# A decoder of four layers: row maxima of two attention cores taken one group and three tiles ahead of the scores, not two groups

## The reference, cut to what matters

```python
scores = einsum('bhqd,bhkd->bhqk', q, k) / sqrt(16)       # 512 x 1024 a head
weights = softmax(scores, axis=-1)
ctx = einsum('bhqk,bhkd->bhqd', weights, v)
```

## Time and profile before

| | us |
|---|---|
| median of three runs | 4876.44 (4870.0 to 4876.64) |
| the profiled execution | 4892.19 |
| its span in the trace | 4890.3 |
| `l1x_core`, first maxima to last exponential | 1498.9 to 1905 |
| `l3x_core`, first maxima to last exponential | 4262.6 to 4782 |
| granted TensorE clock, mean | 0.903 |

### The profile page before, as it was taken

The page is one execution under the profiler, slowest core; times in us unless marked ns, Lnnn a source line. Parts: engine busy times, 40 slices in busy tenths (PEclk is TensorE's granted clock), DMA queues, the critical chain, the costliest instruction groups (busy, mean ns, idle before and its releaser), DMA issues. The chain is left out here.

```text
span 4890.3 us, 69700 instructions
## 1 busy us (share of the span) xinstructions
PE 4176.7 (85%) x20384; PEld 1980.6 (41%) x20384; DVE 2875.0 (59%) x6517; ACT 2350.6 (48%) x4572; POOL 1358.3 (28%) x1202
## 2 busy tenths in 40 slices
PE   8679857689788997797988999999998988489986
PEld 6322346377552333483234333333335544222224
DVE  4458574401667884103863378777873256388866
ACT  4337331243233775233664455454552246279993
POOL 0122141212101111111220288787883212101112
PEclk9669978699887999898898999999999999689998
DMA  8445212354133332574335521111210034613421
GB/s 287 114 104 124 57 38 35 128 198 146 40 117 72 67 69 66 201 255 150 78 75 198 186 69 61 62 62 61 76 44 35 10 117 97 150 47 93 99 52 38
DMA packets 332043, 486.58 MB, mean 99 GB/s; under 512 B 84516, under 2 KB 232597, under 8 KB 317253
## 3 DMA queue, kind: packets, MB, share of 16 engines
q1 hardware_dynamic: 321552, 443.63, 32.1%
q0 software_dynamic: 6384, 32.61, 2.2%
q10 hardware_dynamic: 3804, 6.74, 0.4%
HBM read 327.63 MB, written 143.92 MB: 96 GB/s over the span
## 5 line engine op out<-in xcount | busy, mean ns | idle before, releaser
L1391 POOL TENSOR_TENSOR lc_totals<-lc_totals,lc_weights 128x1024 f32<-128x1024 f32 (+1 forms) x320 | 622.9, 1946 | 164.6 <-DVE lc_totals L1340 133.9
L1321 DVE TENSOR_REDUCE lc_part_max<-ps 128x2 f32<-128x1024 f32 x384 | 466.4, 1215 | 222.1 <-PE ps L1166 219.6
L1300 ACT ACTIVATE lc_weights<-ps 128x1024 f32<-128x1024 f32 x384 | 392.9, 1024 | 418.3 <-PE ps L1186 405.0
L1186 PE MATMUL ps<-lc_q,lc_k 64*128 64x512 f32 x1536 | 395.9, 594 | 4.8 <-issue 4.8
L1196 PE MATMUL ps<-lc_weights,lc_v 128*64 128x512 f32 x1536 | 371.8, 605 | 0.0
L866 DVE TENSOR_REDUCE l1x_core_part_max<-ps 128x1 f32<-128x512 f32 x512 | 316.6, 682 | 55.3 <-PE ps L690 55.1
L862 DVE CUSTOM_DVE_ANT_0 l3x_core_unused<-ps,l3x_core_mask_q 128x512 f32<-128x512 f32 x512 | 330.6, 686 | 6.9 <-DVE l3x_core_row_max L870 4.9
L825 ACT ACTIVATE l3x_core_weights<-ps 128x512 f32<-128x512 f32 x512 | 327.0, 693 | 7.6 <-PE ps L758 7.2
L825 ACT ACTIVATE l1x_core_weights<-ps 128x512 f32<-128x512 f32 x512 | 266.1, 604 | 84.1 <-PE ps L758 84.0
L808 ACT ACTIVATE ps<-l3x_core_mask_k 128x512 f32<-128x512 f32 x384 | 270.2, 704 | 35.8 <-DMA l3x_core_mask_k<-in_mask_k 35.8
L690 PE MATMUL ps<-l3x_core_k,l3x_core_q 96*128 96x512 bf16 x512 | 213.9, 419 | 55.0 <-DVE l3x_core_part_max L862 39.9
(11 more groups left out here) (494 smaller groups left out, 8582.3 us busy)
## 6 DMA issues: line engine op xcount, KB each, us to landing
cf_w<-in_L1f_w SPq DMA_DIRECT2D x32, 1024.0 KB, 7.4
lc_k<-latent_k SPq DMA_DIRECT2D x32, 768.0 KB
lc_v<-latent_values SPq DMA_DIRECT2D x32, 768.0 KB, 5.0
latent_k<-feed_staged SPq DMA_DIRECT2D x64, 256.0 KB, 2.4
latent_values<-feed_staged SPq DMA_DIRECT2D x64, 256.0 KB, 2.0
k_heads<-proj_parts SPq DMA_DIRECT2D x40, 384.0 KB, 2.6
q_heads<-proj_parts SPq DMA_DIRECT2D x32, 384.0 KB, 2.6
q_heads<-proj_parts SPq DMA_DIRECT2D x32, 256.0 KB, 3.0
```

Of the source, the lines that this page charges most:

```text
L1186: mm = nc.tensor.matmul(out[j], k_tile[g % RING][strip(j), i * P:(i + 1) * P], q_tile[g % RING][strip(j), :], start=False, stop=True)
L1300: nc.scalar.activation(weights[:, i % TILES, :, :], k.ps[:, B0 + (i % 2) * HEADS:B0 + (i % 2 + 1) * HEADS, 0:nq], ACT.Exp, scale=scale).th ...
L1321: nc.vector.reduce_max(own, k.ps[:, A0:A0 + HEADS, :], AX).then_inc(a_taken, 1)
L1391: nc.gpsimd.tensor_tensor(total, total, own, ALU.add).then_inc(added_by_pool, 1)
```

## The change

`EARLY = 3` for these two stages: `FRONT` is 12 chunks (3 tiles' worth), `TURN` is tile 5. Before the first score the 32 chunks of group 0 and 12 of group 1 are done. At step s of group g chunk 12 + s of group g + 1 follows for s below 20, and chunk s - 20 of group g + 2 from there. The turn of group g + 1 moves from the end of tile 0 to step 22, and negate to step 23; split and `row` move to the end of GpSimd's and SyncE's program for the group. The loads of the mask by queries move from group 1 to group 2 of a batch, and `row` stands before the last of the four loads of the mask by keys in group 3. All other stages run the same instructions in the same order.

```diff
+    EARLY = 3 if small and nkt == 8 else nkt
+    late_row = EARLY < nkt
+    FRONT, TURN = NCH * EARLY // nkt, nkt - EARLY
+
+    def chunks_at(s):
+
+        return [(1 + m // NCH, m % NCH) for m in range(FRONT + s * NCH // NS, FRONT + (s + 1) * NCH // NS)]
...
-                if exists(*later(b, g, 1)):
+                if exists(*later(b, g, 1)) and not late_row:
                     row(*later(b, g, 1))
...
-                if mask is not None and g == groups - 3 and exists(b + 1, 0):
+                if mask is not None and g == groups - (2 if late_row else 3) and exists(b + 1, 0):
                     for qi in range(nqt):
                         sync.wait_ge(a_taken, at(b, groups - 1, NCH + 1, (qi + 1) * NCH // nqt))
                         load_mask_q(b + 1, qi)
...
+                new_mask = mask is not None and g == groups - 1 and exists(b + 1, 0)
+                for i in range(nkt // 2 if new_mask else 0):
+                    if late_row and i == nkt // 2 - 1:
+                        row(*later(b, g, 1))
+                    sync.wait_ge(exp_done, at(b, g, NS, 2 * (i + 1) * heads + 3))
+                    load_mask_k(b + 1, i)
+                if exists(*later(b, g, 1)) and late_row and not new_mask:
+                    row(*later(b, g, 1))
...
-            pass_a(0, 1, range(NCH))
+            pass_a(0, 1, range(FRONT))
...
-                        pass_a(*later(b, g, 2), more[j])
+                        for ahead, n in chunks_at(s):
+                            if exists(*later(b, g, ahead)):
+                                pass_a(*later(b, g, ahead), [n])
+                        if late_row and (i, j) == (TURN, heads - 2) and exists(*later(b, g, 1)):
+                            turn(*later(b, g, 1))
...
-                    if i == 0 and exists(*later(b, g, 1)):
+                    if not late_row and i == 0 and exists(*later(b, g, 1)):
                         turn(*later(b, g, 1))
...
+                        if late_row and (i, j) == (TURN, heads - 1) and exists(*later(b, g, 1)):
+                            negate(*later(b, g, 1))
...
+                if late_row and exists(*later(b, g, 1)):
+                    split_max(*later(b, g, 1))
```

More of the change, by code:

```diff
@@ L421, in attention_stage @@
     inverse_at = [(2 + p, 0) for p in range(4)]
-    def chunks_of(i):
-        some = list(range(i * NCH // nkt, (i + 1) * NCH // nkt))
-        return [some[len(some) * j // heads:len(some) * (j + 1) // heads] for j in range(heads)]
+    EARLY = 3 if small and nkt == 8 else nkt
[3 more added lines that the diff above has]
+        return [(1 + m // NCH, m % NCH) for m in range(FRONT + s * NCH // NS, FRONT + (s + 1) * NCH // NS)]
     assert not seeded or groups * NS % B_BANKS == 0 and groups * NCH % A_BANKS == 0
@@ L745, in group @@
                 for i in range(nkt):
-                    more = chunks_of(i) if exists(*later(b, g, 2)) else [()] * heads
                     qs, ks = queries_of(i), slice(i * P, (i + 1) * P)
@@ L910, in _ @@
             negate(0, 0)
-            maxima(0, 1, range(NCH))
+            maxima(0, 1, range(FRONT))
             def group(b, g):
@@ L915, in group @@
                 for i in range(nkt):
-                    more = chunks_of(i) if exists(*later(b, g, 2)) else [()] * heads
                     for j in range(heads):
                         after = step_after(b, g, i * heads + j)
+                        if late_row and (i, j) == (TURN, heads - 1) and exists(*later(b, g, 1)):
+                            negate(*later(b, g, 1))
                         if after[2] in by_vector and exists(*after[:2]):
                             fill(*after, at(b, g, NS, i * heads + j + 3))
-                        maxima(*later(b, g, 2), more[j])
+                        for ahead, n in chunks_at(i * heads + j):
+                            if exists(*later(b, g, ahead)):
+                                maxima(*later(b, g, ahead), [n])
                         if (i, j) in inverse_at and not small and exists(*before):
                             invert(*before, inverse_at.index((i, j)))
-                    if i == 0 and exists(*later(b, g, 1)):
+                    if not late_row and i == 0 and exists(*later(b, g, 1)):
                         negate(*later(b, g, 1))
@@ L1004, in group @@
                         add_weights(b, g, i)
-                    if small and i == 0 and exists(*later(b, g, 1)):
+                    if small and not late_row and i == 0 and exists(*later(b, g, 1)):
                         split_max(*later(b, g, 1))
```

## The result

| | before | after |
|---|---|---|
| median (4 runs each) | 4875.23 us (4870.0 to 4876.64) | 4845.44 us (4844.51 to 4846.27) |
| profiled execution, its span | 4892.19, 4890.3 | 4844.51, 4842.7 |
| granted TensorE clock, mean | 0.903 | 0.909 |

The ratio is 0.9939, 95% interval 0.9928 to 0.9951: faster by 29.8 us, 24 to 35, where 27.7 were forecast. The profiled executions differ by 47.7 us. Of that only 26.4 lie in the two stages. The profiled execution of before was itself 17 us above its median, and the other stages run the same instructions in both kernels: 7.6 us of the difference are there when `l1x_core` begins (1498.9 against 1491.3).

The account below looks back on a forecast made before the run. VectorE's back-to-back reductions were taken to bound the starts; beside pass A, TensorE was full in `l1x_core`, ScalarE in `l3x_core`. Terms: -12.0 + 1.9 - 15.6 - 2 = -27.7 us, from 4876.4 to 4849, own range 4843 to 4853.

Parts of the forecast that it names:

- Start: Before each stage's first score: 20 chunks of group 1 leave, saving 12.0 us in `l1x_core` and 15.6 in `l3x_core`.
- Beside the scores, `l1x_core`: Five tiles of scores alone become mixed, 2.84 us in place of 2.46: 1.9 us back.
- Beside the scores, `l3x_core`: Five more tiles become mixed at no cost, because ScalarE fills both kinds: 0, nearest bound 0.4 us.
- The row: Next group's row of maxima lands before its first score: 1.3 us to spare in `l1x_core`, 2.1 in `l3x_core`.
- The mask by queries: `l3x_core`, loads now in group 2: first quarter level with VectorE's need at step 20; 0 taken, far end 4 us.
- the crowd: Transfers crowding group 2 of a batch in `l3x_core` make mask, code or row late: 4 to 9 us back.
- The jump back: VectorE's loop jump at group 2 in `l3x_core`: waits shorten without the mask load, 2 us gained, bounds 0 to 9.
- The first: Rival: in `l3x_core` the wait at the jump goes with the load, 7 us more gained, 4842; chance 0.14.
- The second: Rival: transfers in group 2 of `l3x_core` are late, 4 to 9 us back, 4853 to 4858; chance 0.12.
- the third: Rival: the row is late at every group in both stages, 64 us at the slow landing, 4913; chance 0.06.
- The fourth: Rival: TensorE's clock or an unseen wait slows 16 groups by 1.2 us each, 4868, no change; chance 0.06.
- full clock in all steady groups: The prediction's reading of the windows, given as why it saw nothing for a slower TensorE clock.

Follow-up runs that it names:

- only_l3x: The change made in `l3x_core` alone, `l1x_core` left as in the kernel before: 4857.78 us, ratio 0.9967 to before.
- last_quarter_later: The kernel before, with the last quarter of the mask by queries held until well behind VectorE's jump: 4871.45 us, ratio 0.9998.
- experiment 3: The changed kernel with `EARLY = 2` in place of 3, the turn after step 26: 4885.89 us, ratio 1.0028 to before.
- experiment 5: Kernel before with last mask quarter held behind VectorE's jump: 4871.45 us; changed kernel with `l1x_core` loop longer by two or one memsets a step: 4850.32, 4852.7 us.
- experiment 6: Memsets put ahead of VectorE's work in `l3x_core`: 196 in the kernel before, 4876.36 us; 60 in the changed kernel, 4848.15 us.
- two_tiles_early_turn: The changed kernel with `EARLY = 2` in place of 3 and the turn after step 24: 4858.84 us, ratio 0.9956 to before.

## Why the prediction was right, step by step

The step from views to sum held: 4849 forecast, 4845.4 measured, inside the forecast's own 4843 to 4853. By the profiled executions the terms are -12.0 + 2.7 - 15.8 - 1.3 = -26.4 us, where -27.7 were forecast; the medians differ by 29.8, with an interval of 24 to 35. The starts came out as worked out. That the rest of `l3x_core` came to -1.3 against -2 is in part luck: a gain at the jumps that was taken too small and a growth of the groups that was taken as nothing stand against each other.

- **Start.** -12.0 and -15.6 forecast, -12.0 and -15.8 measured in the profile. The price of a chunk of back-to-back maxima, read from two groups of rows, was the whole answer. With each stage changed alone its start shortens by the same 12 and 15.8 us, and with the late turn alone neither start nor sum moves.
- **Beside the scores, `l1x_core`.** +1.9 forecast, +2.7 measured. Mixed tiles kept their 2.84 us. The 0.8 more lies in the first eight tiles, 24.9 us against 23.9, of which more ran at half clock (6.6 us of the scores against 4.3). That isn't clearly the change's: in two kernels whose `l1x_core` is that of before (only_l3x and last_quarter_later) it was 6.2 and 6.1 us, and the eight tiles took 24.8.
- **Beside the scores, `l3x_core`.** 0 was taken, with 0.4 as bound. The mixed group is 28.88 us where it was about 28.7. Over 12 plain groups this is some 2 us, and the term was too small: ScalarE isn't quite all that counts there. It isn't the late turn, since the late turn alone has 28.68 us; it comes with the chunks' new places, and why wasn't found. The first eight tiles take 30.1 us where they took 28.5, and here the half clock reaches 6.7 us or more into the scores in every kernel with the late turn, the late turn alone included, and 4.4 us or less in every one with the old start and turn.
- **The row.** 1.3 and 2.1 us to spare by the sum of the chain, 1.4 and 2.2 by experiment 3. The landing was the 1.7 us of an empty queue, as assumed.
- **The mask by queries.** No wait for it at three tiles, as taken. At five it costs 15.4 us, so the crowd is real and near.
- **The jump back.** -2 forecast. The two intervals with a jump have lost 3.4 us together in `l3x_core` (33.74 and 32.36 before, 31.74 and 30.93 after), the waits themselves 3.5 us. The term was too small, 2 for 3.4, and came by a way that the prediction didn't name: the load, of which the 2 us were a share, has no part in it (experiment 5), and what shortened the wait is what now stands last in the loop (experiment 6). The waits were to be 2 to 3.5 us each and were 1.7. One step of the argument was also loose: it has the masked loop too long by its 384 instructions of maxima alone, which are fewer than the 512 that it gives room for. The whole loop, 626 in the trace, is longer than that.
- **Rivals.** The first (the wait goes with the load) falls. The second and the third are real mechanisms that begin at five and at two tiles. The fourth had a true core, and "full clock in all steady groups" was read from windows that miss the exceptions. The changed kernel has the lower clock for some 3 us behind each jump back (0.51, after 1.8 us in which TensorE is idle) and for longer into the scores than before. Before had it behind the jumps too. By the first eight tiles the longer half clock goes with 1.0 and 1.6 us a stage, not 1.2 us a group: at a seam TensorE idles for 0.70 us only and keeps 1.00.

## What to carry to other kernels

When a stage starts with work that only one engine can do, count how much of it the first result truly needs: the rest can move beside the steady loop where that one engine has time left. The gain is its back-to-back rate, less what the moved work costs on an engine that is full there (here TensorE in `l1x_core`, 2.7 of 12.0 us). A lead has a lower bound (the chain from last producer to first user) and an upper one (what the early work itself needs), and both can be looked for in rows before trying: the lower one came out within 0.1 us, the upper one I didn't add up for five tiles, and it cost 20 us. Keep the seam of two groups on the side of a long block of other work; moving it by two or three chunks cost more here than the whole change had gained.

## What the runs showed of the hardware

- TensorE idle for 1.68 us in the middle of full work came back at a granted clock of 0.53 and then 0.50 for about 3 us, but not each time: of 14 such waits four kept 1.00, and so did idle times of 1.96 and 1.56 us at the jumps of two_tiles_early_turn. Idle for 0.70 us at each seam, or 0.95 us, it kept 1.00 throughout.
- Through the start of a stage, with TensorE busy 7.19 of 8 us on pass A, the granted clock was 0.50, and it rose to 1.00 only 3.7 to 7.4 us into the scores (before and after).
- VectorE's loop of 286 instructions from jump to jump goes back without a wait and without a packet on q14; loops of 415, 543 and 626 wait 1.7 to 3.8 us at each jump. From the jump to the next instruction it is 2.9 to 3.9 us, and how much of that is idle goes by how much work is queued at the jump: 0.1 us with a waiting reduction last, 1.1 to 1.4 us otherwise. Adding 60 or 196 instructions ahead of the loop changes nothing.
- A DMA of 4 KB lands in 1.7 us on an empty queue and had a median of 4.9 to 5.1 us where eight loads stood ahead of it. Moving it to when these were old gave the whole difference back, which is what made a chain of 4.8 us fit.
